# Windowed attention in slots: where the next batch's work stands, how the output is cut, and which engine scales it

## What is computed

```
h = _layernorm(x, axis=-1) * (1 + ca) + sa
q = (h @ Wq.T).reshape(b, l, 16, 16)            # 16 heads of 16
k = (pad(h) @ Wk.T) ;  v = (pad(h) @ Wv.T)      # 32 zero tokens on either side
scores = einsum('blhd,blwhd->blhw', q, k[:, win_idx]) * 0.25   # 64 keys for each query
attn = softmax(scores, axis=-1)
out = einsum('blhw,blwhd->blhd', attn, v[:, win_idx]).reshape(b, l, 256)
x = x + ga * (out @ Wo.T + bo)
```

## Time and profile before

| | us |
|---|---|
| median of 3 runs | 2984.7 (2984.51 to 2994.8) |
| the profiled execution | 2996.69 |
| its span, first to last instruction | 2994.9 |
| mean granted clock of TensorE | 0.924 of full speed |

### The profile page before, as it was taken

The page is one execution under the profiler, slowest core; times in us unless marked ns, Lnnn a source line. Parts: engine busy times, 40 slices in busy tenths (PEclk is TensorE's granted clock), DMA queues, the critical chain, the costliest instruction groups (busy, mean ns, idle before and its releaser), DMA issues. The chain is left out here.

```text
span 2994.9 us, 44209 instructions
## 1 busy us (share of the span) xinstructions
PE 2533.9 (85%) x16472; PEld 2012.8 (67%) x16472; DVE 1790.3 (60%) x3089; ACT 1277.5 (43%) x1879; POOL 764.4 (26%) x858
## 2 busy tenths in 40 slices
PE   4588873599999999899999949999578765899998
PEld 4477663367777777677777738888445544788887
DVE  3587885278676866776767636565333334676564
ACT  0456652165665656565665613333122213233322
POOL 0011112335343533344333211221134332000100
PEclk8799997699999999999999969999789887999999
DMA  2301012243334333433343240100100003000000
GB/s 111 94 26 42 14 30 73 64 118 101 94 99 125 103 91 111 125 93 96 98 127 94 58 150 8 45 31 8 69 30 15 15 30 118 8 24 8 31 8 15
DMA packets 126954, 194.61 MB, mean 65 GB/s; under 512 B 34592, under 2 KB 92960, under 8 KB 122080
## 3 DMA queue, kind: packets, MB, share of 16 engines
q1 hardware_dynamic: 124960, 191.40, 21.1%
q10 hardware_dynamic: 1792, 0.53, 0.1%
HBM read 118.44 MB, written 61.34 MB: 60 GB/s over the span
## 5 line engine op out<-in xcount | busy, mean ns | idle before, releaser
L1249 DVE TENSOR_REDUCE l_negmax<-l_mx 128x1 f32<-128x512 f32 (+3 forms) x608 | 394.6, 655 | 150.2 <-PE l_mx L1598 149.6
L1479 ACT ACTIVATE l_Phi<-l_s 128x1024 fp32r<-128x1024 f32 x288 | 295.2, 1025 | 266.3 <-PE l_s L1618 258.3
L1261 DVE TENSOR_TENSOR l_Plo<-l_s,l_Phi 128x1024 fp32r<-128x1024 f32 x288 | 350.1, 1216 | 13.8 <-ACT l_s L1483 13.2
L1629 PE MATMUL l_o<-l_Phi,l_V 128*128 128x256 f32 x1152 | 309.6, 290 | 7.6 <-ACT l_Osb L1491 3.0
L1616 PE MATMUL l_s<-l_QA,l_KK 128*128 128x512 f32 x576 | 285.8, 496 | 28.2 <-DVE l_Plo L1261 25.2
L1629 PE MATMUL l_o<-l_Plo,l_V 128*128 128x256 f32 x1152 | 302.6, 284 | 0.0
L2253 ACT ACTIVATE m_hidhi<-m_h 128x512 fp32r<-128x512 f32 x168 | 106.2, 632 | 457.4 <-DVE m_h L2111 457.4
L1598 PE MATMUL l_mx<-l_KK,l_QA 128*128 128x512 f32 (+3 forms) x768 | 274.8, 398 | 29.4 <-DMA l_QB<-l_qd 16.9
L1483 ACT ACTIVATE l_s<-l_s 128x1024 f32<-128x1024 f32 x288 | 294.9, 1024 | 0.0
L1629 PEld LDWEIGHTS l_o<-l_Phi,l_V 128*128 128x128 f32 x1152 | 221.6, 192 | 43.5 <-issue 32.3
L1618 PE MATMUL l_s<-l_QB,l_KL 65*128 65x512 f32 x576 | 231.9, 403 | 0.0
(11 more groups left out here) (345 smaller groups left out, 5936.5 us busy)
## 6 DMA issues: line engine op xcount, KB each, us to landing
l_qd<-l_qs SPq DMA_DIRECT2D x256, 128.0 KB, 2.4
l_QA<-l_qd SPq DMA_DIRECT2D x64, 512.0 KB, 4.5
l_QB<-l_qd SPq DMA_DIRECT2D x64, 256.0 KB, 5.3
l_R<-l_rd SPq DMA_DIRECT2D x128, 128.0 KB, 3.0
l_rps<-l_rp SPq DMA_DIRECT2D x128, 64.0 KB, 1.9
m_xb<-xs SPq DMA_DIRECT2D x8, 1024.0 KB, 4.8
w_xb<-in_x SPq DMA_DIRECT2D x4, 1024.0 KB, 7.0
w_Vodd<-w_V SPq DMA_DIRECT2D x8, 512.0 KB, 5.6
```

What stands on the lines that cost most here:

```text
L1249: v.tensor_reduce(negmax[:, n % 2, at + h0:at + h1], piece_of(number, chunk), AX.X, ALU.max, negate=True).then_inc(reduced, 1)
L1261: v.tensor_tensor(Plo[:, s % 3].rearrange("p u h q -> p (u h q)"), S2[s % 2][:, :], Phi[:, s % 3].rearrange("p u h q -> p (u h q)").bitcas ...
L1479: a.activation(Phi[:, s % 3].rearrange("p u h q -> p (u h q)"), S2[s % 2][:, :], ACT.Exp, scale=L_D ** -0.5).then_inc(exped, 1)
L1629: mm = pe.matmul(O[:, odd * 2 * P:(odd + 1) * 2 * P].rearrange("p (j q) -> p j q", j=2), V[:, b % 2, k, 64 - 64 * odd:192 - 64 * odd], src ...
```

## The change

Four edits, all in `windowed_attention` and its plan:

1. The plan has fixed places. The 17 pieces of the next batch stand in slots 0, 0, 1, 2 (the "turn" pieces) and then one in each of slots 2 to 14.
2. An "out" has 128 tokens and not 256, one in every second slot from slot 3 on; it is half as many products, one L611 and one pair L686 and L689 each. It waits for two windows in place of four. SP issues the third store of a batch ahead of the copy of the odd values.
3. Measuring and normalising are cut into pairs of tiles, in slots 8 to 11 and 12 to 15, and this is done two batches ahead (batch 2 in batch 0, batch 3 in batch 1); batch 1's own is done before the first slot.
4. GpSimd does the product into `yT` (`lay_out`, in place of L601 on DVE) and `tokens_low`, in slots 1, 2 and 3. `both` and `r` have two buffers.

```diff
-    OUT_AT, FIRST_AT = 5, 3
+    AT = (0, 0, 1, 2) + tuple(range(2, 15))
+    OUT_AT = 3
...
-        last = {self.OUT_AT + 4 * n: ("out", n // 4, n % 4) for n in range(4 * B)}
         self.slots = {s: [] for s in range(B * NWIN + 2)}
         for b in range(1, B):
-            s = (b - 1) * NWIN + self.FIRST_AT
-            for kind, u in self.HEAD:
-                while len(self.slots[s]) + (s in last) >= 2:
-                    s += 1
-                self.slots[s].append((kind, b, u))
+            for (kind, u), at in zip(self.HEAD, self.AT):
+                self.slots[(b - 1) * NWIN + at].append((kind, b, u))
+        for n in range(TT * B):
+            self.slots[self.OUT_AT + 2 * n].append(("out", n // TT, n % TT))
         for s in sorted(self.slots):
-            if s in last:
-                self.slots[s].append(last[s])
             for turn in self.slots[s]:
...
-        part, both = sb("part", [P, 2, 2, WINDOW]), sb("both", [P, 2, 2, WINDOW])
-        r = sb("r", [P, 2, WINDOW])
+        part, both = sb("part", [P, 2, 2, WINDOW]), sb("both", [P, 2, 2, 2, WINDOW])
+        r = sb("r", [P, 2, 2, WINDOW])
...
+                store(b, 2)
                 if b + 1 < B:
                     odd_values(b + 1)
-                store(b, 2)
...
             def normal_out(n):
-                b, w = divmod(n, NWIN)
                 x = O[:, :].rearrange("p (x g h q) -> p x g h q", x=2, g=2, h=2)
                 v.wait_ge(parted, n + 1)
-                if n >= 1:
-                    v.wait_ge(laid_out, n)
-                v.scalar_tensor_tensor(both[:, :, :, :], x[:, :, :, 1, :], parity[:, 1:2], part[:, :, :, :],
+                if n >= 2:
+                    v.wait_ge(laid_out, n - 1)
+                v.scalar_tensor_tensor(both[:, n % 2], x[:, :, :, 1, :], parity[:, 1:2], part[:, :, :, :],
                                        ALU.mult, ALU.add).then_inc(picked, 1)
                 v.wait_ge(picked, n + 1)
-                v.reciprocal(r[:, :, :], both[:, 1]).then_inc(recip, 1)
-                v.wait_ge(recip, n + 1)
-                if b >= 1 and w % 4 == 0:
-                    v.wait_ge(freed_v, plan.after(("out", b - 1, w // 4)))
-                v.tensor_tensor(yT[:, :, w * WINDOW:(w + 1) * WINDOW], both[:, 0], r[:, :, :], ALU.mult)\
-                    .then_inc(laid_out, 1)
+                v.reciprocal(r[:, n % 2], both[:, n % 2, 1]).then_inc(recip, 1)
 
             def output(turn):
-                _, b, i = turn
+                _, b, t = turn
+                n = TT * b + t
                 v.wait_ge(filled, plan.index[turn] + 1)
-                for t in range(2 * i, 2 * i + 2):
-                    n = TT * b + t
-                    if n >= 4:
-                        v.wait_ge(added, n - 3)
-                    ins = v.tensor_tensor(tmp[:, t % 4, :], PJ[:, (t % 2) * C:(t % 2 + 1) * C], bo[:, :], ALU.add)
-                    ins.then_inc(freed_v if t % 2 else biased, 1)
+                if n >= 4:
+                    v.wait_ge(added, n - 3)
+                v.tensor_tensor(tmp[:, t % 4, :], PJ[:, 0:C], bo[:, :], ALU.add).then_inc(freed_v, 1)
...
                 tokens_low(0, u)
+            for pair in range(4):
+                measure(1, pair)
+            aggregate(1)
+            for pair in range(4):
+                normalize(1, pair)
             softmax(0)
             softmax(1)
             for s in range(SLOTS + 2):
@@ -652,17 +645,12 @@
                     softmax(s + 2)
                 if 1 <= s <= SLOTS:
                     normal_out(s - 1)
-                if b + 1 < B:
-                    if w == 0:
-                        measure(b + 1, 0)
-                    elif w == 1:
-                        measure(b + 1, 1)
-                        aggregate(b + 1)
-                    elif w in (2, 3):
-                        normalize(b + 1, w - 2)
-                    elif w in (4, 5):
-                        tokens_low(b + 1, 2 * w - 8)
-                        tokens_low(b + 1, 2 * w - 7)
+                if b + 2 < B and 8 <= w < 12:
+                    measure(b + 2, w - 8)
+                    if w == 11:
+                        aggregate(b + 2)
+                elif b + 2 < B and w >= 12:
+                    normalize(b + 2, w - 12)
...
 
+            def lay_out(n):
+                b, w = divmod(n, NWIN)
+                g.wait_ge(recip, n + 1)
+                if b >= 1 and w % 2 == 0:
+                    g.wait_ge(freed_v, plan.after(("out", b - 1, w // 2)))
+                g.tensor_tensor(yT[:, :, w * WINDOW:(w + 1) * WINDOW], both[:, n % 2, 0], r[:, n % 2], ALU.mult)\
+                    .then_inc(laid_out, 1)
+
+            def tokens_low(b, u):
+                k, half = u % 2, u // 2
+                cols = slice(half * HALF, (half + 1) * HALF)
+                at = slice(PAD + half * HALF, PAD + (half + 1) * HALF)
+                g.wait_ge(freed_a, plan.after(("turn", b, u)))
+                g.tensor_tensor(hTlo[:, k, at], hT[:, k, cols], hThi[:, k, at].bitcast(F32), ALU.subtract)\
+                    .then_inc(lowered, 1)
...
             def add_rows(turn):
-                _, b, i = turn
-                if i == 0:
+                _, b, t = turn
+                if t == 0:
                     g.wait_ge(gload[b % 2], 16 * (b // 2 + 1))
                 g.wait_ge(freed_v, plan.after(turn))
-                for t in range(2 * i, 2 * i + 2):
-                    g.tensor_tensor(tmp[:, t % 4, :], tmp[:, t % 4, :], gate[:, b % 2, :], ALU.mult)\
-                        .then_inc(gated, 1)
-                    g.wait_ge(gated, TT * b + t + 1)
-                    g.tensor_tensor(xb[:, b % 3, t, :], xb[:, b % 3, t, :], tmp[:, t % 4, :], ALU.add)\
-                        .then_inc(added, 1)
+                g.tensor_tensor(tmp[:, t % 4, :], tmp[:, t % 4, :], gate[:, b % 2, :], ALU.mult).then_inc(gated, 1)
+                g.wait_ge(gated, TT * b + t + 1)
+                g.tensor_tensor(xb[:, b % 3, t, :], xb[:, b % 3, t, :], tmp[:, t % 4, :], ALU.add)\
+                    .then_inc(added, 1)
 
             g.wait_ge(consts, 1)
             inverse_root(0)
+            inverse_root(1)
             for s in range(SLOTS + 2):
                 b, w = divmod(s, NWIN)
-                if w == 1 and b + 1 < B:
-                    inverse_root(b + 1)
+                if 1 <= s <= SLOTS:
+                    lay_out(s - 1)
+                if b + 1 < B and 1 <= w < 4:
+                    for u in ((0, 1), (2,), (3,))[w - 1]:
+                        tokens_low(b + 1, u)
+                if w == 11 and b + 2 < B:
+                    inverse_root(b + 2)
...
                 else:
-                    pe.wait_ge(laid_out, NWIN * b + 4 * u + 4)
-                    for i in range(2):
-                        t = 2 * u + i
-                        for c in range(KC):
-                            mm = pe.matmul(bank[:, i * C:(i + 1) * C], yT[:, c, t * P:(t + 1) * P], wo[:, c, :],
-                                           start=(c == 0), stop=(c == KC - 1))
+                    pe.wait_ge(laid_out, NWIN * b + 2 * u + 2)
+                    for c in range(KC):
+                        mm = pe.matmul(bank[:, 0:C], yT[:, c, u * P:(u + 1) * P], wo[:, c, :],
+                                       start=(c == 0), stop=(c == KC - 1))
                 mm.then_inc(filled, 1)
```

More of the change, by code:

```diff
@@ L557, in _, with measure @@
         def _(v):
-            def measure(b, half):
-                if half == 0:
+            def measure(b, pair):
+                if pair == 0:
                     v.wait_ge(xload[b % 3], 16 * (b // 3 + 1))
-                for t in range(4 * half, 4 * half + 4):
+                for t in range(2 * pair, 2 * pair + 2):
                     v.bn_stats(st[:, t, :], xb[:, b % 3, t, :]).then_inc(stats, 1)
@@ L567, in aggregate, with normalize @@
                     v.bn_aggr(mv[:, t, :], st[:, t, :]).then_inc(stats, 1)
-            def normalize(b, half):
-                if half == 0:
+            def normalize(b, pair):
+                if pair == 0:
                     v.wait_ge(rstd_ready, b + 1)
@@ L625, in split @@
                 v.tensor_tensor(lo[:, :, :], w[:, :, :], hi[:, :, :].bitcast(F32), ALU.subtract).then_inc(split_lo, 1)
-            biased = signal("biased")
             v.memset(minus_half[:, :], -0.5).then_inc(consts, 1)
@@ L633, in _ @@
                 v.memset(kT[:, b, :, PAD + T:], 0.0).then_inc(consts, 1)
-            measure(0, 0)
-            measure(0, 1)
+            for pair in range(4):
+                measure(0, pair)
             aggregate(0)
@@ L642, in _ @@
                 split(n)
-            normalize(0, 0)
-            normalize(0, 1)
+            for pair in range(4):
+                normalize(0, pair)
             for u in range(4):
                 tokens_low(0, u)
+            for pair in range(4):
+                measure(1, pair)
+            aggregate(1)
+            for pair in range(4):
```

(1 more changed line is left out.)

## The result

The changed kernel's median is 2958.4 us (2952.6 to 2961.3), beside 2985.6 for the kernel before: a ratio of 0.9902 [0.988, 0.9925], so 27 us or 1.0% faster. The forecast of 2953 is 5 us off and its range holds the time. In a second set of runs the medians are 2990.3 and 2955.2, 35 us apart, and the ratio is 0.9885 [0.9851, 0.9919].

The account below looks back on a forecast made before the run. PE and DVE alternate as the bound, with pieces crowded into ten slots. Gains of 5.7, 11.1, 11.6 and 1.4 in batches 0 to 3 and 2.4 in the tail, less 1.0 for collisions, make 31.2: 2953 us (2945 to 2962).

Parts of the forecast that it names:

- Slots 3 to 13: Six slots with a piece and an "out" at 5.30, five with one piece at 4.30: 53.3; batches 0 and 1: 54.0.
- Slots 14 and 15: Slot 14 is DVE's 3.87 us, slot 15 is 5.2, both with 0.68 more in batches 0 and 1.
- Slots 0 to 2: The "turn" pieces load ACT: 5.6, 4.3 and 5.4 us, with 1.0 for GpSimd's low parts, sum 16.3.
- The clock in batches 1 and 2: Half of some 4 us per batch for stretches at half clock is charged: 2.0 each in batches 1 and 2.
- Batch 3: Six pairs of slots at 9.08 and one bare slot, 58.4, with 1.6 at half clock: 60.0 us, gain 1.4.
- The collisions: GpSimd's new product meets DVE's normalisation in 8 slots: 1.0 us charged, from nothing up to 3.7.
- The tail: Behind the last window, one tile less of work, less 0.3 for the new path: gain 2.4 us.
- The ring: The hand-over ring between engines is the bound, one-piece slots 5.2, the others 5.84: 2976 us; chance 0.09.
- The clock: PE's shorter, spread waits draw the clock down; with 13 more half-clock slots the kernel is at 3009 us; chance 0.05.
- GpSimd in the chain: Less gain: a product takes 0.73 and slot 2's query waits its full 2.6: 2965 us; chance 0.15.
- More gain: PE stays at full clock and slots 0 to 2 cost PE's time only: 17 us more, 2936; chance 0.12.
- signs of being wrong: One-piece slots over 4.6, PE idle over 1 ahead of slot 2's query, or the windows' granted clock under 0.93.

Follow-up runs that it names:

- the bias first: Changed kernel, but in slots 8 to 15 DVE adds the bias of an "out" before it measures or normalises; 2958.4 us, ratio 0.9893.

## Why the prediction was right, and where its steps were not

**Slots 3 to 13: one term right, one too small.** In batch 2 they take 53.97, where 53.3 was forecast. A piece with an "out" is 5.25 (5.30), one piece alone 4.46 (4.30): PE's jobs do not butt against each other as closely as 2.75 + 1.55 had it. In batches 0 and 1 they take 55.8 where 54.0 was forecast, and this is the step that failed: "slots 8, 10 and 12 are at DVE's 4.55 instead". Cut at DVE's L581 they take 5.11, 5.48 and 5.58, but these marks shift with DVE's own work: slot 8 takes 5.11 with the bias first, too, and slot 9 gives most of it back (4.70). Cut at PE's first L838 of each slot, which show where PE loses time, slots 8, 10 and 12 take 4.40, 4.90 and 5.56, against 4.40, 4.42 and 4.42 in batch 2, and with the bias first 4.40, 4.42 and 4.42 in all three batches: slots 3 to 13 are then 53.99, 53.99 and 53.99. I had counted DVE's work in the slot and not what stands behind it in its queue. The bias waits behind measuring, the bank waits for the bias, and PE's next piece for the bank.

**Slots 14 and 15**: 10.1 where 10.5 was forecast, and 8.97 in batch 2 (9.1).

**Slots 0 to 2**: 4.81, 5.92 and 5.47, in all 16.2, where 16.3 was forecast as 5.6, 4.3 and 5.4 with 1.0 for GpSimd. The sum is right by luck. The "out" in slot 1 stands behind a "turn" piece and waits 1.5 us until ACT has taken that one out of the bank, which the sum for slot 1 left out, while slot 0 costs less than ACT's sum. In batch 0, whose slot 1 has no "out", that slot is 3.72, so the missing "out" is worth 2.2 and not 0.3. The 3.0 for the clock there comes out by luck as well. Slots 0 and 2 of batch 0, columns as in the earlier trace rows, and PE in slot 2:

```profile
127.97:134.47 6.50, 5.32 (x72) 4.57 (x72) 2.45 (x2) 5.27 (x9) 0.00 (x0) 0.64 0.00 0
...
138.19:144.92 6.73, 4.71 (x45) 3.68 (x44) 3.89 (x5) 4.30 (x8) 3.57 (x4) 1.00 0.00 1
```

```profile
140.21 0.47 PE L810 MATMUL w_pj<-w_hThi,w_wqhi 128*128 128x512 f32 x1 [2.02 <-POOL w_hTlo L681]
```

Slot 0 is at the lower clock for a part and takes 1.7 more than in batch 1. Slot 2 takes 1.3 more at a granted clock of 1.00: there PE, not held up by an "out" in slot 1, waits for GpSimd's two low parts. That wait, 2.0, is over the 1 that the prediction named as a sign of being wrong; in batches 1 and 2 the low parts are done just in time.

**The clock in batches 1 and 2**: "I take half, 2.0 each". All of it came back. The trace of the edit-4 kernel in the old plan has 0.93 and 0.94 there, as before (0.96 and 0.93 in the second trace of before), and every kernel with the new plan 1.00, with or without edits 2 and 4, so it is edits 1 and 3 that do this; which of the two was not tested.

**Batch 3**: 59.1 where 60.0 was forecast. A bare slot is 3.72 and not 3.87, since without L601 it is 0.38 shorter (4.10 with edit 4 undone) and not 0.24. Six pairs at 8.96 and one bare slot at 3.72 are 57.5 (58.4), and one slot took 6.84 in place of 5.25, which is the stretch of 1.6 that I had left in. Its windows and rows:

```profile
400.00:404.00 4.00, 2.52 (x28) 1.83 (x28) 3.91 (x5) 2.03 (x3) 0.45 (x1) 0.78 0.17 66
...
404.00:408.00 4.00, 4.00 (x75) 3.11 (x78) 1.29 (x2) 1.83 (x4) 0.00 (x0) 0.79 0.01 4
```

```profile
402.32 2.05 PE L825 MATMUL w_pj<-w_wo,w_yT 128*128 128x256 f32 x4 [1.16 <-POOL w_yT L673]
```

The four products take 2.05 in place of 1.10, at the lower level (the granted clock of 402.3 to 404.4 is 0.50).

**The collisions**: 1.0 was charged, and 0.4 is seen. GpSimd's new product:

```profile
L673 POOL TENSOR_TENSOR w_yT<-w_both,w_r x64: 452/457/471, 137.2 to 444.7; 128x128 f32<-128x128 f32 x64
```

and DVE's normalisation (ns least, median and most):

```profile
L572 DVE TENSOR_SCALAR w_xn<-w_xb,w_mv,w_rstd x32: 315/408/553, 91.5 to 291.0; 128x256 f32<-128x256 f32 x32
```

All 64 products lie within 20 ns. In each of the eight slots where one meets a pair of normalisations, the second of the pair takes 0.55 in place of 0.41 and the pair 0.78 in place of the 0.73 that it has with edit 4 undone: 0.05, eight times. Nothing in these 64 slots looks like the 0.77 in place of 0.29 of the earlier trace rows. The Trainium skill's lock ("SBUF — State Buffer", section "Who interferes with whom") is not taken by a DVE instruction with at most one SBUF input outside a two-port mode; L601, which reads PSUM and one SBUF tile, agrees, as its 23 meetings with the product leave it at 0.36. The 3.7 that was at stake by the rule in full is not there. But collisions are possible in this plan: with the bias first, L572 beside GpSimd's L689 takes 0.82 in place of 0.41 (the rows of that run above). The warning of "Perfetto Trace Analysis" in the Trainium skill (section "Optimizing Scalar/DVE Operations") that work moved between the two engines might not help holds for the old plan (+0.4 in batches 0 to 2) but not for the new one (-9.3). The old plan has collisions both ways, two L601 of 0.77 before and, with edit 4, two L575 of 0.81 in place of 0.41 beside GpSimd's L697. They changed place, and the new wait of 7.9 for the low parts is far larger.

**The tail**: 2.4 was forecast, 0.6 is there (24.15 to 23.59). It has one tile less, but slot 63 now holds a lone "out": from L590 to L590 it takes 4.91, where the slot took 2.33 before. Of these 2.6 the term had only the 0.95 of the product. In the second trace of the changed kernel the tail is 24.95, so the term is within the scatter.

**The sum.** 33.5 less in the windows, where 29.8 was forecast (the sum without the tail and the rest): 0.6, 0.7, 1.6 and 0.9 too much time in the four batches. The errors are of both signs: in batches 1 and 2 the clock's two times 2.0 was too much, slots 3 to 13 were 1.8 and 0.7 too little. The mechanism was right (with the pieces laid evenly and the measuring done early, PE's wait for scores and the low clock that goes with it are gone), but that a batch comes out within 1 us is partly because mis-sized terms cancel. The median came within 5 us by scatter as well: 31.7 off the old median was forecast, the phase gained 34.2 in the traces, and the program 27.2 in one set of runs and 35.1 in the other.

**The rivals.** *The ring* would have had slots of 5.2 and 5.84: refuted by 4.46 and 5.25. *The clock* did not fall in batches 0 to 2: refuted there, though in batch 3 it was 0.97, 0.94 and 0.91 in three traces, the last under the 0.93 that the prediction gave as a sign. *GpSimd in the chain* is true where an "out" stands alone, which the forecast had in its 4.88. PE's waits in the window of batch 3:

```profile
PE w_pj L825 <- POOL w_yT L673: 8.1, 7, 1.2
```

It does not reach slots 3 to 13, as doubling the product showed. Its low parts did hold up slot 2 of batch 0. This rival's own figure is off: 10 and 15 more give 2963 and 2968, not 2965. *More gain* is half true: its clock came, its shorter slots 0 to 2 did not. Of the signs of being wrong, one-piece slots over 4.6 came in slots 10 and 12 of batches 0 and 1 (4.90 and 5.56 at PE's marks), for the reason given above.

## What to carry to other kernels

When work on a shared bank is spread evenly, look at who frees the bank and what stands ahead of that instruction on its own in-order queue: here the short addition behind other work of DVE cost PE 6.8 us of waiting (15.6 with edit 4 undone), and moving it ahead took 5.5 of the 6.8 away. Look at the durations after such a move, too: here it brought GpSimd's work beside DVE's normalisations, which took 1.23 in place of 0.73. Work that waits for a slow helper goes behind the independent work of its engine, not ahead of it (1.16 of waiting became 0.15), and to cut it into halves doubles how often the wait is paid (8.1 in place of 4.6 us in batch 3). Two edits are to be costed together where one sets what bounds the other: taking work off DVE gave nothing in batches 0 to 2 of the crowded plan and 9 us in the even one.

## What the runs showed of the hardware that was not expected

**Short stretches at the lower clock in batch 3.** The granted clock of batch 3 was 0.97, 0.94 and 0.91 in three traces of the changed program or its first phase, 0.89 with edit 4 undone, 0.89 with the bias first and 0.92 with the doubled product. With GpSimd's product and lone "outs" behind `weigh` or of 256 tokens it was 1.00 in all five traces, while the kernel before had 0.97, 1.00 and 0.95. Each stretch costs 1.2 to 1.6 us, so that this batch varies from one execution to the next by more than some of the edits are worth. Why some kernels and executions show them was not settled.

**The latent phase scatters.** Its code is the same in all, yet it took 1256.5 and 1255.3 in the two traces of the kernel before, 1247.6 and 1247.3 in those of the changed one, and between 1249.6 and 1259.5 in the other kernels. The pairs repeat within 1.2 and 0.3, as the rival in the expectations had it, but the kernels that share the changed plan do not stay near 1247. A difference of single executions of the whole program holds this; the medians less the first phase are 2576 to 2585 for all kernels with four or more runs. What sets it stays open.

**GpSimd's products** take 0.458 for 128 columns, 0.73 for 256 and 1.275 for 512, with hardly any scatter, in line with the estimate of 0.46.

**A pair of DVE's normalisations** takes 0.73 alone, 0.78 when GpSimd's product starts just ahead of the second, and 1.23 when GpSimd's L689 runs beside it.
